# Windowed attention with a gated feed-forward layer: gates and v repeated by transfers through memory

## The reference, cut to what matters

```python
def _window_attend(xh, qkv_w, lepe_w, bias, sp, heads, scale):      # sp = 4, 8 heads of 4 channels
    qkv = jnp.einsum('oi,bihw->bohw', qkv_w, xh)
    q, k, v = jnp.split(qkv, 3, axis=1)
    lepe = jax.lax.conv_general_dilated(v, lepe_w, (1, 1), 'SAME', feature_group_count=c)
    q, k, v, lepe = map(part, (q, k, v, lepe))                      # windows of 4x4 pixels
    attn = jnp.einsum('nhqc,nhkc->nhqk', q * scale, k) + bias[None]
    attn = jax.nn.softmax(attn, axis=-1)
    out = jnp.einsum('nhqk,nhkc->nhqc', attn, v) + lepe

# x = x + conv(_ln_c(x)): each half of the channels, once as it is and once rolled by 2 pixels; the results added
# t = t + ffn(_ln_t(t)), per pixel:
    router_probs = jax.nn.softmax(x @ router_w + router_b, axis=-1)      # 8 experts
    top_p, top_i = jax.lax.top_k(router_probs, K)                        # K = 2
    top_p = top_p / jnp.sum(top_p, axis=-1, keepdims=True)
    expert_out = jnp.einsum('bnd,edc->bnec', x, expert_w) + expert_b
    return jnp.einsum('bnk,bnkc->bnc', top_p, jnp.take_along_axis(expert_out, top_i[..., None], axis=2))
```

## Time and profile before

| | us |
|---|---|
| median of three runs | 3803.37 |
| the profiled execution | 3802.88 |
| its span, first to last instruction | 3801.0 |
| PE busy | 3274.6 (86%) |
| DVE busy | 3207.6 (84%) |
| POOL busy | 2920.3 (77%) |
| ACT busy | 2223.4 (58%) |

### The profile page before, as it was taken

The page is one execution under the profiler, slowest core; times in us unless marked ns, Lnnn a source line. Parts: engine busy times, 40 slices in busy tenths (PEclk is TensorE's granted clock), DMA queues, the critical chain, the costliest instruction groups (busy, mean ns, idle before and its releaser), DMA issues.

```text
span 3801.0 us, 207759 instructions
## 1 busy us (share of the span) xinstructions
PE 3274.6 (86%) x83621; PEld 1990.9 (52%) x83621; DVE 3207.6 (84%) x7044; ACT 2223.4 (58%) x4516; POOL 2920.3 (77%) x5385
## 2 busy tenths in 40 slices
PE   3889898888888888888888988888888898889985
PEld 1655555555555555555555555555555555555541
DVE  2789988888888888988888888888888888999983
ACT  2666655665656656565566665666565665666641
POOL 3988878787878777878787877787787878888860
PEclk8999999999999999999999999999999999999985
DMA  1232323232323222323222232322232323233221
GB/s 32 59 81 73 82 70 82 70 82 68 83 70 80 71 76 76 78 75 78 72 74 78 74 78 72 80 75 78 69 81 69 82 71 82 73 84 79 76 65 39
DMA packets 307856, 279.35 MB, mean 73 GB/s; under 512 B 122368, under 2 KB 288304, under 8 KB 306864
## 3 DMA queue, kind: packets, MB, share of 16 engines
q1 hardware_dynamic: 140976, 152.09, 15.2%
q0 software_dynamic: 165888, 113.57, 12.0%
HBM read 95.33 MB, written 56.62 MB: 40 GB/s over the span
## 4 chain that ended last, share of the span: by engine, by line
PE 25%; SPq 22%; DVE 20%; issue 16%; DMA 10%; ACT 5%; DVEq 1%; POOL 1%; POOLq 0%; ACTq 0%
SPq L401 14%; SPq L433 7%; PE bank L629 6%; DMA z2t<-z 6%; DVE lepe L929 4%; DMA z<-fin 4%; PE bank L584 3%; PE bank L634 3%; PE bank L561 3%; DVE fin L989 3%; PE bank L656 3%; DVE gx L917 2%; PE bank L543 2%; DVE prob L949 2%; ACT row_inv L701 2%
## 5 line engine op out<-in xcount | busy, mean ns | idle before, releaser
L490 POOL DMA_DIRECT2D vx<-vt x3072 | 1555.3, 515 | 623.8 <-issue 487.2
L629 PEld LDWEIGHTS bank<-probT,vx 128*32 128x32 f32 x36864 | 827.9, 191 | 254.1 <-issue 250.4
L629 PE MATMUL bank<-probT,vx 128*32 128x16 f32 x36864 | 888.7, 235 | 25.2 <-issue 23.6
L479 POOL DMA_DIRECT2D kx<-k_sb x1536 | 737.8, 488 | 119.3 <-ACT k_sb L748 100.3
L561 PEld LDWEIGHTS bank<-kx,qx 32*32 32x32 f32 x36864 | 571.6, 109 | 330.6 <-issue 326.9
L561 PE MATMUL bank<-kx,qx 32*32 32x64 f32 x36864 | 673.8, 221 | 54.3 <-issue 46.1
L929 DVE SCALAR_TENSOR_TENSOR lepe<-vpad,lepe_sb,lepe 128x384 f32<-128x384 f32 x960 | 675.8, 704 | 0.0
L917 DVE TENSOR_TENSOR gx<-bank,yn_pair 128x384 f32<-128x384 f32 x768 | 424.2, 552 | 280.6 <-PE bank L532 277.6
L543 PE MATMUL bank<-gx,expert_sb 128*64 128x384 f32 x1536 | 343.1, 526 | 173.2 <-DVE gx L917 171.3
L725 ACT ACTIVATE prob<-prob 128x512 f32<-128x512 f32 x576 | 359.8, 625 | 199.3 <-DVE prob L949 189.9
L509 POOL TENSOR_TENSOR lepe_p<-lepe_p,tap_sb 128x384 f32<-128x384 f32 x384 | 424.7, 1106 | 27.5 <-issue 6.1
(11 more groups left out here) (101 smaller groups left out, 4803.6 us busy)
## 6 DMA issues: line engine op xcount, KB each, us to landing
vx<-vt POOLq DMA_DIRECT2D x3072, 12.0 KB, 1.9
kx<-k_sb POOLq DMA_DIRECT2D x1536, 24.0 KB
yn_pair<-yn POOLq DMA_DIRECT2D x384, 96.0 KB
z<-fin SPq DMA_DIRECT2D x1344, 24.0 KB
xs<-in_x SPq DMA_DIRECT2D x96, 192.0 KB
xt<-in_x SPq DMA_DIRECT2D x192, 96.0 KB
z0t<-z SPq DMA_DIRECT2D x192, 96.0 KB
out_y<-y_out SPq DMA_DIRECT2D x192, 96.0 KB, 2.2
```

The source lines that it names most:

```text
L479: pool.dma_start(kx[to + m:to + C:4, r % 2, m, :], k_sb[at + m:at + C:4, r % 2, :])\
L490: pool.dma_start(vx[to:to + TOK, r % 2, g * 8 + x:g * 8 + 8:2, odd, :], vt[at:at + TOK, r % 2, x::2, :, :].rearrange("p h n k -> p h (n k)"))\
L629: last = MM(bank_o[32 * c:32 * c + 32, at * TOK:(at + 1) * TOK], vx[:, kr % 2, :, at % 2, at // 2 * 4 + c], probT[:, kr % 2, at, c * TOK:( ...
```

## The change

**Gates.** The constant `expert_sel`, the bf16 parts and the eight `spread_gate` matmuls go. The gates stay float32 (17 steps instead of 22); PE transposes them into `bank_g`, ACT copies them to `gateT` (16 rows). SP stores these 24 KB into the internal memory `gate_rows` (slot 39), waits at slot 41 until they have landed and until the tile before has been multiplied, and issues four transfers, each of which reads four rows of 384 values 64 times over, into `gate_wide` (393 KB each, 1.57 MB per tile). DVE then makes four products of 2x384 values per tile, each for two experts and both operands in SBUF, in slots 44 to 46; PE's expert matmuls follow one slot later. The bias is one float32 matmul.

**Lags.** The two additions of y stand in slots 28 and 29 (27 before) and `y` has four buffers. All that follows is later; the output is at slot 47 instead of 39. The logits go to `bank_g` instead of `bank_o`.

**v.** Instead of 16 transfers from `vt` to `vx` POOL issues two stores at slot 6, one slot after DVE's transposition, into the internal memory `v_rows` (128 partitions x 4 rows of 192 bytes each), and at slot 8, when these have landed, eight loads of 48 KB each, which read whole rows with the zeros between them. `v_rows` is cleared once at the start, by four stores.

```diff
-    centre=0, variance=1, value=2, query_key=3, spread_k=4, turn_v=5, place_bias=6, spread_v=8, ...
-    store_z=15, load_tile=24, tile_sum=27, tile_variance=28, router=29, logits=30, gates=31,
-    pair_yn=31, gap_exp=33, turn_gates=34, experts=35, tile_out=39)
+    centre=0, variance=1, value=2, query_key=3, spread_k=4, turn_v=5, store_v=6, place_bias=6, spread_v=8, ...
+    store_z=15, load_tile=24, y_first=28, y_second=29, tile_sum=30, tile_variance=31, router=32, logits=33,
+    take_logits=34, gates=36, gap_exp=37, turn_gates=38, pair_yn=38, store_gates=39, spread_gates=41,
+    expert_bias=43, products=44, experts=45, tile_out=47)
...
+PRODUCT_AT = {(0, 1): 0, (1, 0): 1, (1, 1): 2, (2, 0): 3}
+EXPERT_AT = {(0, 0): 0, (1, 0): 1, (1, 1): 2, (2, 0): 3}
...
+                if ti := s.tile("store_gates"):                                  # SP
+                    wait_alone(sp, gateT_saved, k + 1)
...
+                    sp.dma_start(gate_rows[r % 2], gateT[:, r % 2, :]).then_inc(gate_stored[r % 2], 16)
+                if ti := s.tile("spread_gates"):
+                    wait_alone(sp, gate_stored[r % 2], (k // 2 + 1) * 16)
+                    if s.later(r, 1):
+                        wait_alone(sp, gx_made, k * PAIRS)
+                    by_expert = gate_rows[r % 2].rearrange("(f p e) n -> e f p n", f=2, e=2)
+                    for odd in range(2):
+                        for half in range(2):
+                            sp.dma_start(gate_wide[odd * C:(odd + 1) * C, :, half, :],
+                                         by_expert[odd, half].unsqueeze(0).broadcast_to([C, PAIRS, SPX]))\
+                                .then_inc(gate_spread[r % 2], 16)
...
+                if st := s.strip("store_v"):                                     # POOL
+                    wait_alone(pool, vt_made, k + 1)
...
+                    for x in range(2):
+                        pool.dma_start(v_rows[r % 2, x, :, x::2, :],
+                                       vt[:, r % 2, x::2, :, :].rearrange("p h n k -> p h (n k)"))\
+                            .then_inc(v_stored[r % 2], 16)
                 if st := s.strip("spread_v"):
-                    wait_alone(pool, vt_made, k + 1)
+                    wait_alone(pool, v_stored[r % 2], (k // 2 + 1) * 32)
...
-                            for odd in range(2):
-                                pool.dma_start(vx[to:to + TOK, r % 2, g * 8 + x:g * 8 + 8:2, odd, :],
-                                               vt[at:at + TOK, r % 2, x::2, :, :].rearrange("p h n k -> p h (n k)"))
+                            pool.dma_start(vx[to:to + TOK, r % 2, :, g * 8:(g + 1) * 8, :].rearrange("p o q n -> p o (q n)"),
+                                           rows).then_inc(v_spread[r % 2], 16)
...
-                    MM(bank_g[:, 0:SPX], expert_sel[:, e, :], gateT[:, r % 2, :], start=True, stop=True)
...
-                    for part in range(3):
-                        MM(bank_f[:, 0:SPX], ebias_part[:, part, :], gateT[:, r % 2, :], start=(part == 0), stop=(part == 2))
+                    MM(bank_f[:, 0:SPX], ebias_sb[:, :], gateT[:, r % 2, :], start=True, stop=True)
...
-                    V.tensor_tensor(gx[:, e % 4, :], bank_g[:, 0:SPX], yn_pair[:, r % 2, e % 2, :], ALU.mult)
+                    V.tensor_tensor(gx[:, p % 2, :, :], gate_wide[:, p, :, :], yn_pair[:, r % 2, :, :], ALU.mult)
```

More of the change, by code:

```diff
@@ L239, in metaformer_block @@
         z2t = sb("z2t", [128, 2, SPX])
-        y = sb("y", [128, 2, SPX])
+        y = sb("y", [128, 4, SPX])
         yn = sb("yn", [128, 2, SPX])
@@ L357, in _ @@
                         .then_inc(const_loaded, 16)
-                    for part in range(3):
-                        sp.dma_start(ebias_sb[part * GE + half * E:part * GE + (half + 1) * E, rows], expert_b)\
-                            .then_inc(const_loaded, 16)
+                    sp.dma_start(ebias_sb[half * E:(half + 1) * E, rows], expert_b).then_inc(const_loaded, 16)
             x_flat = x.rearrange("b c r w -> b c (r w)")
@@ L469, in _ @@
             pool.wait_ge(spread_cleared, N_SPREAD_CLEARED)
+            for ring in range(2):
+                for x in range(2):
+                    pool.dma_start(v_rows[ring, x].rearrange("p q n -> p (q n)"), kx[:, 0, 0, :]).then_inc(rows_cleared, 16)
+            pool.wait_ge(rows_cleared, 4 * 16)
             def slot(s):
@@ L623, in slot @@
                             pe.wait_ge(log_made, k)
-                    if ti := s.tile("gates"):
-                        pe.wait_ge(logit_saved, ti[0] + 1)
                     for w in range(UW):
@@ L704, in slot @@
                     act.wait_ge(gateT_made, k + 1)
-                    S.activation(gateT[0:3 * GE, r % 2, :], bank_p[0][0:3 * GE, 0:SPX], ACT.Copy).then_inc(gateT_saved, 1)
+                    if s.later(r, 2):
+                        act.wait_ge(expert_made, (k - 1) * PAIRS)
+                    S.activation(gateT[:, r % 2, :], bank_g[0:GE, 0:SPX], ACT.Copy).then_inc(gateT_saved, 1)
                 if st := s.strip("variance"):
@@ L856, in gate_step_of @@
                     dve.wait_ge(gate_step, k * (GATE_STEPS - 2) + (at if at < GATE_SPLIT else at - 1))
+                if at == 14 and s.later(r, 1):
+                    dve.wait_ge(gateT_made, k)
                 best, src, hot = (best1, logits[:, :], one1) if at < 6 else (best2, rest2, one2)
@@ L905, in slot @@
-                ex = s.in_tile("experts")
+                            gate_step_of(s, working[0], working[1], at)
+                ex = s.in_tile("products")
                 def gate_product(place):
-                    e = ex and EXPERT_AT.get((ex[2], place))
-                    if e is None:
+                    p = ex and PRODUCT_AT.get((ex[2], place))
+                    if p is None:
                         return
                     k, r, _ = ex
-                    dve.wait_ge(gate_spread, k * E + (e + 1))
-                    if e == 0:
+                    if p == 0:
+                        dve.wait_ge(gate_spread[r % 2], (k // 2 + 1) * (GATE_DMAS * 16))
@@ L950, in slot @@
                                     over_keys(row_max[:, r % 2, :]), ALU.subtract).then_inc(shifted, 1)
-                gate_work((0, 0), (7, 8), (12, 13))
+                gate_work((1, 2), (12, 13))
+                gate_product(0)
+                if yt := s.tile("tile_out"):
+                    k, r = yt
+                    dve.wait_ge(expert_made, (k + 1) * PAIRS)
+                    if s.later(r, 2):
+                        dve.wait_ge(out_stored[r % 2], k // 2 * 32)
+                    V.tensor_tensor(y_out[:, r % 2, :], bank_f[:, 0:SPX], y[:, r % 4, :], ALU.add).then_inc(y_out_made, 1)
                 if st := s.strip("divide"):
```

197 lines of the change are left out of this document (76 added, 121 removed).

## The result

The changed kernel takes 3777.59 us (median of 14 runs, 3753.06 to 3800.47) against 3804.72 of the kernel before (14 runs). The ratio is 0.9935, 95% interval 0.9908 to 0.9961: 25 us less by the ratio and 27 by the medians, where 324 were forecast, and outside the range of 3330 to 3720. The direction holds, by a hair more than what can be told from nothing.

A forecast was written before the change was run, and what follows sets the result against it. It took SP's issues and waits as the bound: 37.8 us per tile falling to 34.4 over 92 tile periods saves 313 us, both ends 10 more, giving 3480 us with 2 us around the span; range 3330 to 3720.

The forecast's parts named there:

- The waits that were to go: DVE's waits per tile for repeated gates (2.9 us, line 532) and z2t (1.2), and PE's waits (3.8), would vanish.
- The old loop from `fin` over z2t: Loop through SP's z stores and loads, DVE's y and the next `fin`: 37.8 us per tile, would become 32 at most.
- SP's additions: Gate store issue 0.6 us, its landing 2.0, four spread issues 2.8, two waits 0.1: 5.5 us more SP work per tile.
- Its sum of 34.4 us: SP's work per tile: 28.9 us before the change plus 5.5 us added.
- Rival (d): SP can't issue a spread transfer until the queue takes the previous one: 40.6 us per tile, 4060 us; chance 0.14.
- The rule of the Trainium skill ("DMA: Bandwidth & Descriptors", Specifications): v's 192-byte stores, under 512 bytes, would take two to three times as long, about 5 us of transfer per tile more.
- The pace is then set by SP: SP busy without pause at 34.4 us per tile; DVE (33) and PE (31) wait for it a little.
- long transfers, but no limit: Data queues: 10.3 us per tile plus gates' 6.0 and v's loads and stores makes 18 to 20 us, not binding.
- By that rule: POOL's SBUF reads block DVE's two-SBUF-operand instructions, so the new products could wait; the sum took them as free of it.
- POOL bounds nothing in either case: POOL saves 6.2 us of issues per tile; even v stores at 2 us each, adding 6, would not make it binding.
- Its waits go, 3.8 us: PE loses its waits, 3.8 us per tile, and eight gate matmuls, 2.7, coming to 31.3 us.
- Rival (b): DVE's products blocked by POOL's additions and crowded transfers take back half the gain: 36.2 us per tile, 3650 us; chance 0.18.

The follow-up runs named there:

- e5: Changed kernel with gate transfers carrying 64 of 384 pixels (result wrong elsewhere) and ACT copying q before the slot's exponential and bias: 3551.78 us, 0.9329.
- e10: Kernel before with only v's way through memory, and POOL's additions narrowed to 8 of 384 columns (part of the convolution left out): 3562.2 us, 0.9349.
- e9: Kernel before with POOL's additions narrowed to 8 of 384 columns (part of the convolution left out): 3607.92 us, 0.9483.
- e3: Changed kernel with the four gate transfers carrying 64 of 384 pixels, same issues and waits (result wrong elsewhere): 3600.08 us, 0.9451.
- e8: Changed kernel with the four gate transfers issued between slot 42's z stores, same bytes; products, expert matmuls and output one slot later: 3675.67 us, 0.9662.
- e7: Changed kernel with POOL's additions narrowed to 8 of 384 columns (part of the convolution left out): 3687.75 us, 0.9667.
- e2: Kernel before with only v's way through memory added: 3842.38 us, 1.0081.
- e1: Changed kernel with v's old 16 scatter transfers back, so only the gates go through memory: 3722.05 us, 0.9784.
- e4: Changed kernel with ACT copying q out of PSUM before the slot's exponential and bias: 3730.65 us, 0.9813.
- e15: e5 with POOL's additions also narrowed to 8 of 384 columns (both omissions make the result wrong): 3502.31 us, 0.9195.
- e11: Changed kernel with v's old scatter, gate transfers between z stores, q copied first, and the gates' landing awaited behind the first z store: 3620.35 us, 0.9504.

## Why the prediction was wrong

Right steps, by its own parts:

- The waits that were to go went. The old loop from `fin` over z2t is nearly off the chain (SP 5%, transfers 2%), and DVE has no line 532 to wait for.
- SP's additions: 0.32 + 2.2 + 2.67 us against 0.6 + 2.0 + 2.8. Its sum of 34.4 us was met by 36.0 in e5, where alone it set the pace; the missing 1.6 us are mostly the five x loads, 3.0 to 3.5 us instead of the 2.26 taken, and the seven loads of a tile, 5.0 to 5.6 instead of 4.45.
- The product on its own: 0.949 us at the median against 0.95.
- Rival (d) is out: a spread issue takes 0.62 us at the median, 2.1 at most. The rule of the Trainium skill ("DMA: Bandwidth & Descriptors", Specifications) on pieces under 512 bytes had no visible effect: in e10 the packets of these stores move 4224 bytes in 262 ns at the median, 16 bytes per ns, those of the old scatter 768 in 44, 17.5, and e10 is faster than e9.

The step that failed is "The pace is then set by SP: it is busy without a pause, 34.4 us". SP waits 3.4 us per tile for `fin`, and a tile takes 37.8 us. Four terms under it were missing or at nothing:

1. "The transfers [...] That is 18 to 20 us of 34: long transfers, but no limit." The mean was right (53% of the time, 20 us of 38). But 1.57 MB come in one burst that fills all engines for 8 us, and there PE's next instructions, which are brought by transfers too, are late. The prediction priced transfers only by what waits for their data. e3 puts 178 us on the bytes of the gates and e8 102 us on their being issued in one row.
2. "By that rule [...] my sum has them free of it." The lock was named and left out because the second addition of y mostly escapes it. The products are 0.14 us above their median in the mean, 55 us of DVE's time, and the taps, which the prediction hadn't looked at, 0.08 us longer each than before, 79 us. That is why DVE's busy time fell by 24 us and not by the 1.6 us per tile of the forecast. It is not the whole of the missing gain, though: removing the lock gives 90 us here (e7) but 197 in the kernel before (e9), whose 3801 us, the start of the sum, had it in already. POOL's additions don't stand still against DVE when POOL's other work changes.
3. "POOL bounds nothing in either case." POOL's busy time did fall by 513 us, but its freedom has no worth, and the way of v costs 31 us in e2, there by the new moments of its additions (e10), and 56 us in the changed kernel against e1, where that wasn't separated from the fuller transfers and the clock. The edit was costed at nothing because nobody waited for POOL; what it does to others while it works was not asked.
4. "Its waits go, 3.8 us", PE at 31.3. PE got other waits: 194 us for ACT's copies of q. The loop of each strip over PE, ACT and DVE was nowhere in the sum, which had added busy times. It is worth 47 us (e4). PE also ran at a lower granted clock (0.902 against 0.943), so that its instructions cost more where it had waited: 132 more of the 384 centre matmuls took 0.91 us than before. No run holds the clock fixed, so its price stays open.

So the place was right where the first and the last of these costs were absent (e5, short transfers and q first), and in the changed kernel SP waits 3.4 us per tile for work that they delay. That the time fell at all, as forecast, is in part luck: without POOL's additions the same change costs 80 us (e7 against e9). Rival (b) had both mechanisms, products under the lock and crowded transfers, and gave 3650 (3680 by its own terms: 32.1 and 4.4 us are 36.5, not 36.2); it was too small because it priced each on a single instruction, the product and z's landing, while the lock falls on the taps too and the crowding on PE's instructions. The parts don't add up: from 3778 the four cuts of e3, e4, e7 and of e1 give 178 + 47 + 90 + 56 = 371 us by themselves, e15, which has three of them (without e1's), is 275 us faster instead of their 315; and e4's 47 us vanish beside e1. They share one loop, and each cut uncovers the next. That PE's instructions wait in the queue is inferred from the transfers that begin after PE has stopped and from e3 and e8; no row shows a transfer being asked for.

## What to carry to other kernels

Price a large transfer also by what shares its engines in its few microseconds: look at the transfers' share slice by slice at the place where it is issued, and break it into pieces between other issues. Ask of each engine that is freed not only who waits for it but whose instructions it blocks, and measure the instructions that the change does not touch. When a wait on a long loop goes, add up the next shorter loops too, over all engines that a strip passes, not only the busy time of each engine.

## What the hardware showed

- Within a run of equal small matmuls, PE stands still, for 0.85 us in the mean in the kernel before and 1.7 in the changed one, at places that all lie 1.0 to 2.5 us behind the end of a 16 KB instruction transfer: 53 us in all in the kernel before, 208 in the changed one, 54 with short gate transfers. The instruction transfer takes 1.12 us at the median in both kernels; what is late is its beginning.
- Narrowing POOL's 384 additions speeds the kernel before by 197 us (e9). DVE's normalisation of y takes 0.52 us, or 2.17 where it overlaps an addition of POOL (e2). A product with one operand in PSUM takes 0.55 us either way (kernel before).
- A centre matmul of 128x384 float32 takes 0.54 us in the mean at the granted clock's higher level and 0.91 at the lower (changed kernel).
- PE's product with v takes 235 ns with the old layout of `vx` and 214 with the new one (kernel before, changed kernel).
- To issue a store of 512 rows of 192 bytes takes POOL 0.813 us, against 0.515 for 64 rows; the upper bound of 2 us was far off.
- With the wait for a landing moved behind another wait and one store of 0.8 us, SP waited 26 us for it (e11) instead of 167 (e8).
